# Eight-expert layer: the second projection as three float16 products of high and low parts

## The reference

```python
logits = xf @ Wg
top_v, top_i = jax.lax.top_k(logits, TOP_K)          # TOP_K = 2
top_w = jax.nn.softmax(top_v, axis=-1)
h1 = jnp.einsum('nd,edf->enf', xf, W1)
h3 = jnp.einsum('nd,edf->enf', xf, W3)
y = jnp.einsum('enf,efd->end', jax.nn.silu(h1) * h3, W2)   # the second projection
y = jnp.transpose(y, (1, 0, 2))
sel = jnp.take_along_axis(y, top_i[:, :, None], axis=1)
out = jnp.sum(sel * top_w[:, :, None], axis=1)
...
x = x + jnp.tanh(g_ffn[1]) * _L1_ffn_ref(_layernorm(x, axis=-1), L1_ffn_Wg, L1_ffn_W1, L1_ffn_W3, L1_ffn_W2)
```

## Time and profile before

| what | value |
|---|---|
| median of 3 runs | 6253.56 us |
| span of the profiled execution | 6259.8 us, 6.2 above the median |
| busy: TensorE products, TensorE loads, VectorE, ScalarE, GpSimd | 5618.2, 4179.0, 4496.2, 2969.0, 1850.6 us |
| mean granted TensorE clock | 0.957 of full speed |
| the stage of the change | about 1673 to 2871 us of the span |
| its 4096 records of `down` (L933) | 478.2 us busy, 275 ns each |
| its 3072 products of `up` (L923) | three groups of 389 us busy, 380 ns each |
| its 512 gates (L1008) | 350.8 us busy, 691 ns each |
| its 512 silu (L960) | 305.7 us busy, 597 ns each |

### The profile page before, as it was taken

The page is one execution under the profiler, slowest core; times in us unless marked ns, Lnnn a source line. Parts: engine busy times, 40 slices in busy tenths (PEclk is TensorE's granted clock), DMA queues, the critical chain, the costliest instruction groups (busy, mean ns, idle before and its releaser), DMA issues. The chain is left out here.

```text
span 6259.8 us, 144526 instructions
## 1 busy us (share of the span) xinstructions
PE 5618.2 (90%) x44938; PEld 4179.0 (67%) x44938; DVE 4496.2 (72%) x11034; ACT 2969.0 (47%) x6074; POOL 1850.6 (30%) x2211
## 2 busy tenths in 40 slices
PE   7887989999899999998888899888899879998888
PEld 5665668888766666665666666577677657776544
DVE  7887867777655555546888676798888678998544
ACT  4554755555433333333555454455555345555344
POOL 3332001101000000002333333677777643332300
PEclk9998989999999999998999999999999889999988
DMA  0000000000100000000000000000000000000000
GB/s 31 2 2 5 1 12 6 5 5 5 40 4 1 1 1 1 1 1 4 2 2 2 12 0 0 9 0 0 0 0 0 5 8 2 2 2 2 5 11 17
DMA packets 47081, 33.23 MB, mean 5 GB/s; under 512 B 37816, under 2 KB 40056, under 8 KB 46460
## 3 DMA queue, kind: packets, MB, share of 16 engines
q1 hardware_dynamic: 46848, 30.20, 1.8%
HBM read 25.98 MB, written 4.19 MB: 5 GB/s over the span
## 5 line engine op out<-in xcount | busy, mean ns | idle before, releaser
L960 ACT ACTIVATE l1f_silu<-l1f_h 128x512 f32<-128x512 f32 x512 | 305.7, 597 | 808.1 <-PE l1f_h L923 806.9
L1008 DVE TENSOR_TENSOR l1f_gated<-l1f_h,l1f_silu 128x512 f32<-128x512 f32 x512 | 350.8, 691 | 283.5 <-ACT l1f_silu L960 277.2
L933 PEld LDWEIGHTS l1f_y<-l1f_w,l1f_gated 128*128 128x128 f32 x4096 | 477.4, 192 | 20.2 <-DVE l1f_gated L1008 1.9
L933 PE MATMUL l1f_y<-l1f_w,l1f_gated 128*128 128x128 f32 x4096 | 478.2, 275 | 1.4 <-DVE l1f_gated L1008 1.4
L923 PE MATMUL l1f_h<-l1f_xhi,l1f_hi 128*128 128x512 f16 x1024 | 389.1, 380 | 29.0 <-DVE l1f_gated L1008 19.9
L923 PE MATMUL l1f_h<-l1f_xlo,l1f_hi 128*128 128x512 f16 x1024 | 389.3, 380 | 0.0
L923 PE MATMUL l1f_h<-l1f_xhi,l1f_lo 128*128 128x512 f16 x1024 | 389.3, 380 | 0.0
L1604 POOL TENSOR_TENSOR l3a_probs<-l3a_probs,l3a_later 128x512 f32<-128x512 f32 x256 | 320.5, 1281 | 4.9 <-DVE l3a_total L1792 4.9
L1590 POOL TENSOR_TENSOR l3a_keys<-l3a_kT,head 128x2048 f32<-128x2048 f32 x64 | 230.4, 3600 | 233.6 <-ACT l3a_kT L1717 233.6
L562 POOL TENSOR_TENSOR l1f_ve<-l1f_mv,eps 128x4 f32<-128x4 f32 x16 | 4.2, 263 | 989.5 <-DVE l1f_mv L552 989.5
L1024 DVE SCALAR_TENSOR_TENSOR l1f_acc<-l1f_y,l1f_route,l1f_acc 128x128 f32<-128x128 f32 x448 | 126.1, 344 | 237.2 <-PE l1f_y L933 237.2
(11 more groups left out here) (477 smaller groups left out, 17779.0 us busy)
## 6 DMA issues: line engine op xcount, KB each, us to landing
l1f_w<-in_L_W SPq DMA_DIRECT2D x16, 256.0 KB, 3.2
out_x<-x_res SPq DMA_DIRECT2D x16, 256.0 KB, 2.0
x_res<-in_x SPq DMA_DIRECT2D x1, 3840.0 KB, 12.3
l1x_pair_ctx<-in_ctxT SPq DMA_DIRECT2D x128, 19.2 KB
l1f_w<-in_L_W SPq DMA_DIRECT2D x1, 2048.0 KB, 9.9
l0x_ctxT<-in_ctxT SPq DMA_DIRECT2D x64, 19.2 KB, 2.0
l1x_ctx<-in_ctx SPq DMA_DIRECT2D x64, 19.2 KB
l2x_ctxT<-in_ctxT SPq DMA_DIRECT2D x64, 19.2 KB, 2.0
```

What stands on the lines that cost most here:

```text
L933: last = pe.matmul(ps_y[e % 2][:, j * P:(j + 1) * P], gated[e % 2][t][:, j * P:(j + 1) * P], w2[:, e, t, :], start=(t == 0), stop=(t == FT ...
L960: act.activation(silu[c % 2][:, :], ps_1[c % 2][:, :], ACT.Silu, scale=SPLIT ** -2).then_inc(s_silu, 1)
L1008: dve.tensor_tensor(gated[e % 2][t][:, :], ps_3[t % 2][:, :], silu[t % 2][:, :], ALU.mult).then_inc(s_gated, 1)
```

## The change

The second projection gets the form of the first. The gate now writes `gated` without the factor SPLIT^2. ScalarE rounds it to float16 (`ghi`; new step `high`, once per quarter, in its queue behind the silu of the next quarter). GpSimd computes the remainder `glo` = `gated` - `ghi`, also float16 (new step `rest`, once per quarter). `w2` is split once, scaled by SPLIT, into `w2hi` (ScalarE) and `w2lo` (VectorE), in the first iteration. `down` waits for `glo`, and each of its 16 products becomes three float16 products: ghi by w2hi, ghi by w2lo, glo by w2hi. The route weights take out 1/SPLIT. On TensorE `down` moves one step back, behind `up` 2, and on VectorE `collect` moves behind gate 2.

```diff
--- before.py
+++ after.py
@@ -878,6 +878,9 @@
         hi, lo = st.sb("hi", [P, E, 2, F], F16), st.sb("lo", [P, E, 2, F], F16)
         silu = st.sb2("silu", [P, GROUP * P])
         gated = [[st.sb(f"gated{i}{t}", [P, GROUP * P]) for t in range(FT)] for i in range(2)]
+        ghi = [[st.sb(f"ghi{i}{t}", [P, GROUP * P], F16) for t in range(FT)] for i in range(2)]
+        glo = [[st.sb(f"glo{i}{t}", [P, GROUP * P], F16) for t in range(FT)] for i in range(2)]
+        w2hi, w2lo = st.sb("w2hi", [P, E, FT, P], F16), st.sb("w2lo", [P, E, FT, P], F16)
         acc = st.sb("acc", [P, GROUP * P])
         ps_xT, ps_lg = st.ps("xT"), st.ps("lg")
         ps_1, ps_3, ps_y = [[st.ps(f"{k}{i}") for i in range(2)] for k in ("h1", "h3", "y")]
@@ -885,6 +888,7 @@
         rt = Router(st, g, E, fr, ps_lg, wg)
         s_g, s_w13, s_w2 = st.sem("s_g"), [st.sem(f"s_w13{e}") for e in range(E)], st.sem("s_w2")
         s_whi, s_wlo = st.sem("s_whi"), st.sem("s_wlo")
+        s_w2hi, s_w2lo, s_ghi, s_glo = [st.sem(k) for k in ("s_w2hi", "s_w2lo", "s_ghi", "s_glo")]
         s_up, s_silu, s_gated, s_y, s_acc, s_x = [st.sem(k) for k in ("s_up", "s_silu", "s_gated", "s_y", "s_acc", "s_x")]
 
         with nc.Block() as block:
@@ -902,7 +906,18 @@
             @block.gpsimd
             def _(pool):
                 rt.make_before(pool)
-                skewed(pool, n, [(lambda it: fr.inverse_deviation(pool, it), 0)], 2)
+
+                def rest(it, c):
+                    e, t = c // FT, c % FT
+                    pool.wait_ge(s_ghi, nth(it, T, c))
+                    if (due := nth(it, E, e, back=2)) is not None:
+                        pool.wait_ge(s_y, due)
+                    pool.tensor_tensor(glo[e % 2][t][:, :], gated[e % 2][t][:, :], ghi[e % 2][t][:, :],
+                                       ALU.subtract).then_inc(s_glo, 1)
+
+                steps = [(lambda it, c=c: rest(it, c), 2) for c in range(T)]
+                steps.insert(4 * FT, (lambda it: fr.inverse_deviation(pool, it), 0))
+                skewed(pool, n, steps, 6)
 
             @block.tensor
             def _(pe):
@@ -924,20 +939,22 @@
                     last.then_inc(s_up, 1)
 
                 def down(it, e):
-                    pe.wait_ge(s_gated, nth(it, T, e * FT + FT - 1))
+                    pe.wait_ge(s_glo, nth(it, T, e * FT + FT - 1))
                     if (due := nth(it, E, e, back=2)) is not None:
                         pe.wait_ge(s_acc, due)
-                    pe.wait_ge(s_w2, 16)
+                    pe.wait_ge(s_w2lo, 1)
                     for j in range(GROUP):
+                        cols = slice(j * P, (j + 1) * P)
                         for t in range(FT):
-                            last = pe.matmul(ps_y[e % 2][:, j * P:(j + 1) * P], gated[e % 2][t][:, j * P:(j + 1) * P],
-                                             w2[:, e, t, :], start=(t == 0), stop=(t == FT - 1))
+                            for k, (x, w) in enumerate(((ghi, w2hi), (ghi, w2lo), (glo, w2hi))):
+                                last = pe.matmul(ps_y[e % 2][:, cols], x[e % 2][t][:, cols], w[:, e, t, :],
+                                                 start=(t == 0 and k == 0), stop=(t == FT - 1 and k == 2))
                     last.then_inc(s_y, 1)
 
                 steps = []
                 for e in range(E):
                     us = [(lambda it, e=e, t=t: up(it, e, t), 2) for t in range(FT)]
-                    steps += us[0:2] + [(lambda it, e=(e - 1) % E: down(it, e), 2 + (e < 1))] + us[2:4]
+                    steps += us[0:3] + [(lambda it, e=(e - 1) % E: down(it, e), 2 + (e < 1))] + us[3:4]
                     if e == 1:
                         steps.append((lambda it: fr.turn(pe, it), 1))
                     if e == 3:
@@ -960,9 +977,21 @@
                     act.activation(silu[c % 2][:, :], ps_1[c % 2][:, :], ACT.Silu,
                                    scale=SPLIT ** -2).then_inc(s_silu, 1)
 
+                def high(it, c):
+                    e, t = c // FT, c % FT
+                    if first_of(it) and c == 0:
+                        act.wait_ge(s_w2, 16)
+                        act.activation(w2hi[:, :, :, :], w2[:, :, :, :], ACT.Copy, scale=SPLIT).then_inc(s_w2hi, 1)
+                    act.wait_ge(s_gated, nth(it, T, c))
+                    if t == 0:
+                        if (due := nth(it, E, e, back=2)) is not None:
+                            act.wait_ge(s_y, due)
+                    act.copy(ghi[e % 2][t][:, :], gated[e % 2][t][:, :]).then_inc(s_ghi, 1)
+
                 steps = []
                 for c in range(T):
                     steps.append((lambda it, c=c: silu_(it, c), 2))
+                    steps.append((lambda it, c=(c - 1) % T: high(it, c), 2 + (c < 1)))
                     if c == 2 * FT + 1:
                         steps.append((lambda it: fr.fetch(act, it, s_up, T), 1))
                     if c == 5 * FT + 1:
@@ -991,7 +1020,7 @@
                     dve.wait_ge(rt.s_out, nth(it))
                     dve.tensor_tensor(rt.act_in[:, :, :], rt.act_out[:, :, :], rt.sel[:, :, :], ALU.mult)
                     dve.drain()
-                    rt.reciprocal_of_sum(dve, rt.act_in, times=SPLIT ** -2)
+                    rt.reciprocal_of_sum(dve, rt.act_in, times=1.0 / SPLIT)
                     if (due := nth(it, E, ago=2)) is not None:
                         dve.wait_ge(s_acc, due)
                     dve.tensor_tensor(rt.w[it.par][:, :, :], rt.act_in[:, :, :], rt.wide(rt.one), ALU.mult).then_inc(rt.s_w, 1)
@@ -1005,7 +1034,12 @@
                     if t == 0:
                         if (due := nth(it, E, e, back=2)) is not None:
                             dve.wait_ge(s_y, due)
-                    dve.tensor_tensor(gated[e % 2][t][:, :], ps_3[t % 2][:, :], silu[t % 2][:, :], ALU.mult).then_inc(s_gated, 1)
+                    dve.scalar_tensor_tensor(gated[e % 2][t][:, :], ps_3[t % 2][:, :], SPLIT ** -2, silu[t % 2][:, :],
+                                             ALU.mult, ALU.mult).then_inc(s_gated, 1)
+                    if first_of(it) and c == 0:
+                        dve.wait_ge(s_w2hi, 1)
+                        dve.scalar_tensor_tensor(w2lo[:, :, :, :], w2[:, :, :, :], SPLIT, w2hi[:, :, :, :],
+                                                 ALU.mult, ALU.subtract).then_inc(s_w2lo, 1)
 
                 def collect(it, e):
                     dve.wait_ge(s_y, nth(it, E, e))
@@ -1035,7 +1069,7 @@
                 steps = [(lambda it: fr.normalize(dve, it), 1)]
                 for e in range(E):
                     gs = [(lambda it, e=e, t=t: gate(it, e, t), 2) for t in range(FT)]
-                    steps += gs[0:2] + [(lambda it, e=(e - 1) % E: collect(it, e), 2 + (e < 1))] + gs[2:4] + between.get(e, [])
+                    steps += gs[0:3] + [(lambda it, e=(e - 1) % E: collect(it, e), 2 + (e < 1))] + gs[3:4] + between.get(e, [])
                 skewed(dve, n, steps, 6)
 
 
```

## The result

The changed kernel takes **6376.28 us** (median of four runs, 6373.45 to 6383.03), beside 6253.69 us for the kernel before on the same chip (6252.54 to 6254.78): a ratio of 1.0193, with a 95% interval of 1.0179 to 1.0208. It is slower by 122.6 us, where 76 was forecast.

A forecast was written before the change was run, and what follows sets the result against it. TensorE was taken to bound the kernel, busy 196 of 200 us. Products −7.0, stalls +9 and clock +1.5 gave +3.5 per iteration; times 16 is 56, and 20 once: +76, 6330 us (8 in 10: 6205 to 6430).

The forecast's parts named there:

- products: In down, 48 float16 products of 56.2 ns replace 16 float32 ones: 2.70 us for 3.57, −7.0 us per iteration.
- lost cover: VectorE's norm and router work ahead of gate 0' is no longer hidden by down: 3.7 us per iteration at least.
- GpSimd's share of the stalls: GpSimd's remainders and VectorE's two-operand work take turns, raising the stalls from 3.7 to 9 us per iteration (5.8 to 11.5).
- clock: TensorE runs at 1.2 GHz behind idle gaps of some 3 us: 1.5 us per iteration, one place of up to three.
- once: First-iteration w2 split 8, W1 and W3 splitting some 10, last down 2: 20 us in all (12 to 30).
- rival 2: In down, weight loads limit the float16 stream to 84 ns a pair: +3.7 us per iteration, 6501 us; chance 0.06.
- the regular stall of 0.37: TensorE's wait of up for the gate two steps back, per expert: unchanged by the new order, nothing won or lost.
- the normalisation: VectorE's work ahead of expert 0, four of 0.34 us: stall 0.4 us, or 0.4 to 2.9 with GpSimd's turns.
- rival 1: GpSimd blocks nothing in this stage, only lost cover counts: −3.3 us per iteration, 6216 us; chance 0.25 with its neighbours.
- Who goes first: Between experts, VectorE was to start first at 1.44 us, GpSimd's remainder at 1.50, 0.18 us behind ScalarE's end.
- The addition: VectorE's addition, placed after expert 0 in the prediction's count: no stall, 0 us.
- Rival 3: GpSimd's remainder is late for down, four plain experts waiting 1.3 us each: 83 us more, 6413 us; chance 0.10.

The follow-up runs named there:

- e2: Kernel before, its own order, with 48 float16 products of constant tiles per expert in place of down's float32 products; second projection left out: 6151.83 us.
- e1: Kernel before with only the order of TensorE and VectorE changed, down and collect one step later, products still float32: 6335.62 us.
- e3: Changed kernel without GpSimd's subtraction; the low part is a constant zero and down waits for the rounding: 6235.99 us.
- e5: Changed kernel with the old 2+2 order, and down starting on rounded parts, waiting for the last remainder only ahead of its 12th product: 6273.66 us.
- e6: Changed kernel with the old 2+2 order on TensorE and VectorE (down and collect behind the second up and gate): 6352.69 us.
- e4: Changed kernel with GpSimd's remainder replaced, same place and waits, by a sum of 4 columns and one memset: 6239.06 us.

## Why the prediction was right, and where its sizes were off

The sign and the mechanism held; the result lies inside the range and 46 us above the forecast. Per iteration, +3.5 was forecast, and +7.1 came: every cost of the steady part was taken too low. Cover and GpSimd's share together are 11.6 us, where 9 was taken from bounds of 5.8 and 11.5. That the end came out no further off is partly luck: the once-only part was smaller than forecast, and 15 steady iterations counted instead of 16.

| term | predicted | measured | by |
|---|---|---|---|
| products | −7.0 | −7.13 | e2, `down` 28.57 to 21.44 |
| lost cover | +3.7 | +5.1 | e1 |
| GpSimd's share of the stalls | +5.3 (9 less 3.7) | +6.5 | changed less e3, without the clock |
| clock | +1.5 | +2.6 | lower clock 5.51 against 0.26, half of it |
| sum | +3.5 | +7.1 | |
| once | +20, beside 16 iterations | +15, beside 15 | below |

- **Products.** 56.2 ns were worked out from the line between 65 and 512 columns, 55.8 were measured. The bound of 84 ns and with it rival 2 are out: loads are hidden in a stream of 48 as in one of 12. The Trainium skill's rule of about 81 ns per pair (TensorE: Matmul & The Clock Gate, Back-to-back issue gap) isn't borne out by this trace: 55.8 ns, with a load for every product.
- **The order.** The step that failed is "the regular stall of 0.37 stays as it is: nothing won or lost". The stall stays, but TensorE's own turn and scores had stood in its place: they showed as 0.07 and 0.44 us before and show as 0.44 and 0.85 now. That is 0.8 us per iteration in no term of the sum. It is read from the lengths, not tested apart. The second miss is the normalisation, 1.0 for 0.4: its row has 10.6 us of idle by issue ahead of it, up to 2.9 us at a turn of VectorE's loop, and `down` had hidden that. In e1 this run is 5.55 to 6.01 us in nine of the 13 iterations and 8.50 to 8.75 in the four others, and only the first kind is what the 0.4 stood for. I had cited the row for its duration and passed over its idle column.
- **GpSimd.** That the engines take turns was right, and rival 1 is out; its own case, a kernel in which nothing is blocked, is e3 at 6235.99, where it was priced 6216; in the changed kernel the blocking costs 9.2 us per iteration. Who goes first was wrong: ScalarE's end to GpSimd's start is 0.08 us here, where 0.18 was taken from the earlier trace rows, so that GpSimd is ahead of L601 by 0.06 us, instead of behind it by as much, and the first two-operand instruction loses as well. The remainder itself takes 1.15 us, where 1.27 was taken. Behind experts 4, 5 and 6 the stalls were 9.21 − 5.55 = 3.7, 3.2 and 2.0 us with the clock in them: the first two are above the upper ends given (3.4, 2.9), the third is below its own (2.3).
- **The addition** behind expert 7 was costed at nothing. It is under the cover in e1 (5.55), and 0.87 over it in the changed kernel, since L1065 takes 1.65 us for 0.74 beside a remainder. The step that failed asked whether the addition's own length was covered, and didn't ask it again of the lengthened one.
- **Clock.** It is at the lower level for 5.51 us per iteration, in stretches of some 3.4 us: 1.6 places, where one was assumed. Of the 2.6 us that this is estimated to cost, 1.6 show in `down` alone (23.07 for 21.44).
- **Once.** The first `collect` is 12.0 us late and the first iteration 5.5 us longer than a steady one, of 18 predicted for both. The largest of it is one wait:

```profile
1703.61 0.58 PE L938 MATMUL l1f_h<-l1f_xhi,l1f_hi 128*128 128x512 f16 x1 [7.89 <-DVE l1f_gated L1037]
```

 Ahead of it stand w2's rounding, 3.61 us, and its remainder, 4.43; 5 and 5.4 were the upper bounds. From the first to the last `collect` row is 113.2 us more, and 122.6 − 12.0 − 113.2 = −2.6 is left for the end: behind the last of these rows stand no router work for a next iteration and none of its stalls, where a whole +3.5 and 2 for the last `down` had been counted. The two traces have it too: the last of VectorE's instructions in the stage starts 59.9 us behind the last of these rows (2992.5), where it was 63.0 (2870.4). So 12.0 + 5.5 − 2.6 = 15 us are once, and 15 steady iterations bring the other 108.
- **Rival 3** is absent from the changed kernel: 3.5 us in all, and 0.2 us of slack were enough, since a remainder is shorter than taken. e5 and e6 showed it alive one step of the order away.

## What to carry to other kernels

Work that an added engine makes longer costs only where a reader waits behind it. So before an engine is given new work, look up which instructions run beside it and what is queued behind them, and place the lengthened work where the result behind it is not needed for a while. An operand that becomes ready by two engines in a row should stand in each of their queues ahead of anything that waits for TensorE. When an order is changed to hide a new latency, list all that the old order hid, idle by issue included: here the new order cost 81 us, and it took the moving of VectorE's work (183 us) to make the change a gain.

## What the runs showed of the hardware

- GpSimd's 128x512 subtraction, which reads two tiles, held back VectorE's instructions with two tiles to read in SBUF (L601 0.68 to 1.65 us, L695 0.42 to 1.38), by 0.97 and 0.96 us beside its own 1.15. GpSimd memsets of 525 and 312 ns at the same places did not (684 ns). By the Trainium skill (SBUF — State Buffer, Who interferes with whom) a VectorE instruction with two inputs in SBUF contends with GpSimd's reads and not with its writes; these runs agree. Not expected was what the subtraction does to small ones: L1021, 128x32, took 1.15 us for 0.18. What reads PSUM (the gate, 689 ns; `collect`, 344; L648, 178) didn't move. Of those that read one small tile of SBUF, the reduction L657 stayed at 0.19 us and the `TENSOR_SCALAR` L679 went from 0.17 to 0.68; why these two differ wasn't tried.
- A memset did lengthen `TENSOR_SCALAR` instructions with one input: L575 from 342 to 410 ns, and to 502 with two memsets; L705, 128x32, from 181 to 443 and 691. The subtraction does it too, and a reduction is left alone: in e6 L703 took its usual 0.42 us from 2308.68, beside a remainder that ran from 2308.79 to 2309.94, and L705 behind it took 0.81 for 0.18.
- Idle stretches of TensorE of 2.7 to 2.8 us within dense work were followed by the lower clock for some 3.4 us (0.66 on average from 2318.00 to 2321.50) in 21 of 26 cases in iterations 3 to 15 of the changed kernel, and in five not (the one of 2.81 us at 2328.34 is such a case). In e4 one of 2.13 us was followed by it and one of 2.39 wasn't. In e1, whose longest wait for a gate is 1.9 us, none of the stage's steady part was at the lower level.
